# Graph attention on one core: the edge mask multiplied into the centred scores ahead of the exponentials, instead of uniform weights added by products of their own

## What is computed

```python
q = (x @ Wq + bq).reshape(N, H, HEAD)
k = (x @ Wk + bk).reshape(N, H, HEAD)
v = (x @ Wv + bv).reshape(N, H, HEAD)
scores = jnp.einsum('nhd,mhd->nhm', q, k) / np.sqrt(HEAD)
adj = jnp.zeros((N, N), jnp.float32).at[edge_index[0], edge_index[1]].set(1.0)
scores = jnp.where(adj[:, None, :] == 0, -1000000000.0, scores)
attn = jax.nn.softmax(scores, axis=1)
attn_out = jnp.einsum('nhm,mhd->nhd', attn, v).reshape(N, D_OUT)
attn_out = attn_out @ Wo + bo
h1 = _layer_norm(x + attn_out, g1, be1)
ff = jax.nn.relu(h1 @ W1 + b1) @ W2 + b2
```

## Time and profile before

| | before |
|---|---|
| device time, median of 3 runs | 234.52 us (234.5 to 235.0) |
| device time of the profiled execution | 235.3 us |
| its span, first to last instruction | 232.4 us |
| PE busy | 222.9 us, 96% |
| DVE busy | 176.1 us, 76% |
| ACT busy | 127.1 us, 55% |
| POOL busy | 5.5 us, 2% |
| mean granted TensorE clock | 0.995 |

### The profile page before, as it was taken

The page is one execution under the profiler, slowest core; times in us unless marked ns, Lnnn a source line. Parts: engine busy times, 40 slices in busy tenths (PEclk is TensorE's granted clock), DMA queues, the critical chain, the costliest instruction groups (busy, mean ns, idle before and its releaser), DMA issues.

```text
span 232.4 us, 3302 instructions
## 1 busy us (share of the span) xinstructions
PE 222.9 (96%) x1212; PEld 181.1 (78%) x1212; DVE 176.1 (76%) x318; ACT 127.1 (55%) x236; POOL 5.5 (2%) x17
## 2 busy tenths in 40 slices
PE   8999999999999999999999999999999999999970
PEld 4985789766766887888888888888888888997860
DVE  2979776767697689875976868878879767987564
ACT  0646489449679636635546646447476544732320
POOL 1000010000000000000000000000000000001001
PEclk9999999999999999999999999999999999999997
DMA  6999999985003927136100000058840000000001
GB/s 219 323 406 395 394 387 405 404 342 185 0 0 127 400 48 119 31 52 110 21 1 3 0 0 1 0 192 315 283 161 0 0 3 1 0 3 0 0 0 45
DMA packets 28614, 31.25 MB, mean 134 GB/s; under 512 B 17948, under 2 KB 18868, under 8 KB 27576
## 3 DMA queue, kind: packets, MB, share of 16 engines
q1 hardware_dynamic: 27808, 30.54, 38.7%
q10 hardware_dynamic: 792, 0.51, 0.8%
HBM read 30.79 MB, written 0.26 MB: 134 GB/s over the span
## 4 chain that ended last, share of the span: by engine, by line
PE 92%; ACT 3%; DVE 1%; issue 1%; POOLq 0%; POOL 0%; DVEq 0%; ACTq 0%
PE bank L745 37%; PE bank L728 13%; PE bank L544 6%; PE bank L535 6%; PE bank L576 4%; PE bank L593 3%; PE bank L755 3%; PE bank L756 3%; ACT C L342 3%; PE bank L620 2%; PE bank L886 1%; PE bank L553 1%; PE bank L704 1%; PE bank L605 1%; PE bank L705 1%
## 5 line engine op out<-in xcount | busy, mean ns | idle before, releaser
L745 PE MATMUL bank<-W2hi,Hhi 128*128 128x512 f32 x128 | 49.8, 389 | 0.0
L745 PE MATMUL bank<-W2hi,Clo 128*128 128x512 f32 x128 | 49.8, 389 | 0.0
L745 PE MATMUL bank<-W2lo,Hhi 128*128 128x512 f32 x128 | 49.8, 389 | 0.0
L435 ACT ACTIVATE Mhi<-M 128x512 fp32r<-128x512 f32 x32 | 20.3, 633 | 44.2 <-DVE M L1142 44.2
L1147 DVE TENSOR_TENSOR Mlo<-M,Mhi 128x512 fp32r<-128x512 f32 x32 | 22.1, 690 | 11.8 <-ACT M L436 11.8
L1142 DVE TENSOR_TENSOR M<-bank,b2r 128x512 f32<-128x512 f32 x32 | 22.0, 687 | 9.5 <-PE bank L756 5.4
L745 PEld LDWEIGHTS bank<-W2hi,Clo 128*128 128x128 f32 x128 | 24.0, 188 | 5.0
L745 PEld LDWEIGHTS bank<-W2hi,Hhi 128*128 128x128 f32 x128 | 24.0, 188 | 5.0
L745 PEld LDWEIGHTS bank<-W2lo,Hhi 128*128 128x128 f32 x128 | 24.0, 188 | 5.0
L428 ACT ACTIVATE Hhi<-C 128x512 fp32r<-128x512 f32 x32 | 20.0, 624 | 11.4 <-DVE C L1128 11.1
L342 ACT ACTIVATE C<-bank,cols 128x512 f32<-128x512 f32 x32 | 19.5, 704 | 10.5 <-PE bank L576 10.5
(11 more groups left out here) (253 smaller groups left out, 337.8 us busy)
## 6 DMA issues: line engine op xcount, KB each, us to landing
F<-in_L_gnn_W SPq DMA_DIRECT2D x2, 2048.0 KB, 19.3
W<-in_L_gnn_W SPq DMA_DIRECT2D x3, 1024.0 KB, 5.4
W1raw<-in_L_gnn_W SPq DMA_DIRECT2D x1, 2048.0 KB, 22.4
ids<-in_src SPq DMA_DIRECT2D x2, 1024.0 KB, 13.0
ids<-in_dst SPq DMA_DIRECT2D x2, 1024.0 KB, 7.1
dst_ids<-in_dst SPq DMA_DIRECT2D x2, 1024.0 KB, 7.6
src_ids<-in_src SPq DMA_DIRECT2D x1, 2048.0 KB, 8.4
Wq<-in_L_gnn_Wq SPq DMA_DIRECT2D x4, 256.0 KB, 3.9
```

What stands on the lines that cost most here:

```text
L435: act.activation(Mhi[:, t, :], M[:, t, :], ACT.Mish)
L745: done = mm(ST2[t][:, :], x[:, c, e], w[:, c, :], start=c == 0 and i == 0, stop=c == KC - 1 and i == 2)
```

## The change

The product of ones and the mask takes the place of the separate uniform weights. The centred scores are multiplied by min(count, 1) before the exponentials: a pair without an edge has eight scores of 0, eight exponentials of 1, a sum of 8 and eight weights of 1/8. `uniform`, `eighth`, the memset, the ACT instruction and the four products with `uniform` go; so does the mask in L1042. The bias products of L637 move ahead of the wait on `v_ready`.

```diff
             act.activation(CTs[:, :], bank[0][:, 0:N], ACT.Copy).then_inc(S["ct_read"], 1)
-            act.wait_ge(S["eighth"], 1)
-            act.activation(uniform[:, :], bank[0][:, 0:N], ACT.Relu, bias=eighth[:, 0:1], scale=-1.0 / HEADS).then_inc(S["uniform_ready"], 1)
             for o in range(2):
                 act.wait_ge(S["s_centred"], o + 1)
...
             turn_features(0)
-
+            for b in range(2):
+                mm(O_BANKS[b][:, 0:D // 2], ones2[:, :], bvo_parts[:, D + D // 2 * b:D + D // 2 * (b + 1)], start=False, stop=False)
             pe.wait_ge(S["v_ready"], 1)
-            pe.wait_ge(S["uniform_ready"], 1)
-            for j in range(KC):
-                mm(quarter(bank[3], j), v_sb[:, P * j:P * (j + 1)], uniform[:, :], start=j == 0, stop=False)
             for o, j in ((o, j) for o in range(2) for j in range(KC)):
                 h = 2 * j + o
                 pe.wait_ge(S["attn_ready"], o + 1)
                 done = mm(bank[3][HEAD * o:HEAD * (o + 1), P * j:P * (j + 1)], v_sb[:, HEAD * h:HEAD * (h + 1)], attn[:, o, j, :],
-                          start=False, stop=j == KC - 1)
+                          start=j == 0, stop=j == KC - 1)
             done.then_inc(S["ao_done"], 1)
-            for b in range(2):
-                mm(O_BANKS[b][:, 0:D // 2], ones2[:, :], bvo_parts[:, D + D // 2 * b:D + D // 2 * (b + 1)], start=False, stop=False)
...
             for o in range(2):
-                v.tensor_tensor(attn[:, o], bank[1 + o][:, :].rearrange("p (j n) -> p j n", j=KC),
-                                total[:, :].unsqueeze(1).to_broadcast([P, KC, N]), ALU.subtract).then_inc(S["s_centred"], 1)
+                centred = v.tensor_tensor(attn[:, o], bank[1 + o][:, :].rearrange("p (j n) -> p j n", j=KC),
+                                          total[:, :].unsqueeze(1).to_broadcast([P, KC, N]), ALU.subtract)
+            chain(centred)
+
+            dve.wait_ge(S["ct_read"], 1)
+            chain(v.tensor_scalar(mask[:, :], CTs[:, :], 1.0, None, ALU.min))
+            for o in range(2):
+                v.tensor_tensor(attn[:, o], attn[:, o], mask[:, :].unsqueeze(1).to_broadcast([P, KC, N]), ALU.mult).then_inc(S["s_centred"], 1)
...
             chain(v.reciprocal(total[:, :], total[:, :]))
-            dve.wait_ge(S["ct_read"], 1)
-            chain(v.scalar_tensor_tensor(out=total[:, :], in0=CTs[:, :], scalar=1.0, in1=total[:, :], op0=ALU.min, op1=ALU.mult))
             for o in range(2):
                 v.tensor_tensor(attn[:, o], attn[:, o], total[:, :].unsqueeze(1).to_broadcast([P, KC, N]), ALU.mult).then_inc(S["attn_ready"], 1)
```

More of the change, by code:

```diff
@@ L79, in gnn_kernel @@
         warm = sb("warm", [P, P], BF16)
-        uniform = sb("uniform", [P, N])
-        eighth = sb("eighth", [P, 1])
         Dg = sb("Dg", [P, GT, N], F32R)
@@ L206, in gnn_kernel @@
                      "out_stored consts ident_ready x_transposed xT_ready cols_done cols_ready q_done k_done v_done "
-                     "qk_ready v_ready onehot_bf ct_done ct_read uniform_ready eighth ea_done ea_hi ea_lo wc_hi wc_lo bvo_in bvo_hi bvo_parts sign_ready scores_done s_centred exp_done attn_ready ao_done ao_hi ao_lo wo_hi wo_lo wo_done "
+                     "qk_ready v_ready onehot_bf ct_done ct_read ea_done ea_hi ea_lo wc_hi wc_lo bvo_in bvo_hi bvo_parts sign_ready scores_done s_centred exp_done attn_ready ao_done ao_hi ao_lo wo_hi wo_lo wo_done "
                      "stat_ready rstd_ready nx_ready nT_done nT_ready f1_done ff_ready f2_done pre_done pre_read late_done late_read "
@@ L314, in _ @@
             pool.memset(mhalf[:, :], -0.5).then_inc(S["consts"], 1)
-            pool.memset(eighth[:, :], 1.0 / HEADS).then_inc(S["eighth"], 1)
             pool.wait_ge(S["consts"], 3)
```

## The result

| | before | after |
|---|---|---|
| device time, median of 22 executions each | 235.03 us (234.23 to 236.06) | 235.34 us (234.84 to 237.47) |
| mean of the same 22 | 235.01 us | 235.94 us |
| profiled execution: device time, span | 235.3, 232.4 us | 235.5, 233.5 us |
| PE busy, DVE busy | 222.9, 176.1 us | 222.1, 177.3 us |

What follows compares the result with a forecast made beforehand. PE was taken to bound the kernel, reached at the attention through ACT's copy of v and the uniform products. DVE's +1.66 - 0.33, less 0.59 slack, plus 0.06 hand-over, gave +0.80: 235.3 us, range 234.7 to 235.9.

Steps and rivals of the forecast that it cites:

- The mechanism inside the span: Attention: added DVE mask work makes weights 1.33 us later and the heads' products on PE 0.80 us later.
- 0.1 more for a cold start of PE: Heads' products: 0.1 us extra when PE resumes behind its new idle stretch.
- upper bound: Attention: half 1 of the weights late by 0.2 us plus 0.1 for PE's cold start; +1.1, or 235.6 us.
- the delay: Heads' products on PE start 0.80 us later, handed on whole to the end; likeliest case, chance 0.75.
- the first rival: Behind the attention: the delay is taken up on the way, as by fixed transfer waits; about 234.6 us, chance 0.16.
- The faster rival: Attention: without uniform PE could start the heads' products 0.69 us earlier, giving 233.8 us; chance 0.05.
- the last of the sum: Whole kernel: the 0.80 us step added unchanged to the median device time, 234.52 + 0.80 = 235.3 us.
- the rival on the clock: Behind PE's 1.5 us idle stretch: clock falls to 1.2 GHz, +2.7 us on top of 0.80, about 238.0; chance 0.04.

Runs made afterwards that it cites:

- e4: The changed kernel with the four products of v and uniform put back, uniform now all zeros; mean device time 235.81 us.
- e5: The changed kernel without the mask's three DVE instructions, so no pair of nodes is masked; mean 233.95 us, ratio to before 0.9948.
- e2: The changed kernel, unchanged, run again beside before; mean device time 236.41 us, ratio 1.0056.
- e1: The kernel before, unchanged, run again as the measure of scatter; mean device time 235.21 us.
- e3: The changed kernel with six matmuls of ones issued while PE waits for the attention weights; mean device time 235.80 us.
- e6: The changed kernel without the softmax maximum, the mask multiplying the scores straight from the banks; mean 234.87 us, ratio to before 0.999.
- e7: The changed kernel without the softmax maximum, and with edges counted ahead of the products for the scores; mean 234.31 us, ratio to before 0.9961.
- e9: The changed kernel with three matmuls of ones issued while PE waits for the attention weights; mean device time 236.18 us.
- e10: The changed kernel with the product by the mask made twice; mean device time 237.74 us.
- e8: The changed kernel without the maximum, edges counted first, and the mask formed before DVE waits for the scores; mean 233.93 us, ratio to before 0.996.

## Why the prediction was right and where it was wrong

**The mechanism inside the span** was right at each station. The times of after, with its 0.26 of late start taken off, against the forecast: exponentials from 18.65 (18.73), reciprocal to 21.48 + 0.95 - 0.26 = 22.17 (22.25), weights from 22.20 (22.28), heads' products from 23.04 (23.03), aoThi from 24.68 (24.65), the feed-forward products from 32.90 (32.9). Two terms were off and cancelled. The mask took 0.23 us, not 0.29, and the two hand-overs around it 0.03 each, not 0.04; the hand-over from DVE to the waiting PE took 0.14, not 0.06. That 0.08 more is all that the runs show of the "0.1 more for a cold start of PE" in the upper bound, for which the prediction had no row. Scores to end grew from 219.0 to 219.85 and the feed-forward products came 0.83 later, where 0.80 was forecast. Nothing behind the scores took the delay up, so the first rival is out as it was put, by a fixed wait on PE's path; e4 shows that the removed products gave nothing back.

**The faster rival** was priced rightly: with no cost on DVE the heads' products start 0.77 earlier (0.69 forecast, e5). Its time, 233.8, came close to e5's 233.95, but by another sum: of the 1.1 us under before's mean 0.3 came from the span's part behind the scores, 0.3 from the time around the span, and the rest, 0.5, is left for the program's start. It also overlooked Wo's landing, which caps the gain.

**The first step that failed** is the last of the sum, "on the median the same step gives 234.52 + 0.80 = 235.3". It hands the 0.80 of the span on to the device time whole, and so puts at nothing, without a reason, what may change around the span and ahead of the scores. The medians of 22 differ by 0.31, and after's lower group is 0.2 above before in the first comparison and level with it in e2's. The time around the span, which no view of the profile holds, is 2.0 in all 34 executions of after and 2.3 to 2.5 on the mean in before: 0.3 to 0.5 back. And after's lower group has a mean span of 233.21, 0.5 to 0.7 above before's means, not 0.83; so some 0.2 to 0.3 must lie ahead of the scores. That is a remainder, which no run isolates, and why the time around the span differs is open too. What the runs do show is that the delay behind the scores is there, 0.83 at the feed-forward products, and that less than a quarter of it is left in the lower group's device time.

**The second step that failed** is the rival on the clock, given a chance of 0.04 on the evidence that "at the end of the kernel PE has no work from 225 on, and the granted clock is still 1.00 in the stretch 229 to 230". That is one execution. In e1, the same kernel, PE's last work ends before 226, and the clock falls in the stretch from 228:

```profile
225.00:226.00 1.00, 0.65 (x6) 0.44 (x4) 0.48 (x2) 0.00 (x0) 0.00 (x0) 1.00 0.00 0
...
227.00:228.00 1.00, 0.00 (x0) 0.00 (x0) 0.96 (x2) 0.00 (x0) 0.54 (x1) 1.00 0.00 0
228.00:229.00 1.00, 0.00 (x0) 0.00 (x0) 0.96 (x2) 0.00 (x0) 0.00 (x0) 0.71 0.00 0
```

So the delay from the last work to the fall varies by 2 us and more between executions of one program. (It is also why before has mean clocks of 0.988 to 0.990 in some executions. In e1's profile, 0.990, the low level from 228.4 to the end accounts for all that is missing, and it hits no matmul.) The place of that rival was right. Its price, +2.7 us, was too high: 0.95 and 0.9 in the two traces that show the fall, 1.9 to 2.0 between the groups. In e2 the fall comes after PE has resumed, so the heads' products take 2.44 us and not twice 1.60, and part of the low level lies in PE's wait for aoThi. Its chance should have been near 0.4 for each execution. It is no alternative to the delay either: it comes on top, in some executions. It adds 15/34 x 1.9 = 0.8 us to after's mean span, as much as the delay itself.

**Luck.** The forecast 235.3 met the median 235.34 because it started from 234.52, the median of the first three times, whose like over 22 is 235.03. And on the means +0.93 looks like the forecast +0.80 only because the two failed steps nearly cancel: +0.83 behind the scores, +0.7 from the clock (8/22 x 2.0), 0.3 to 0.5 back around the span, and the remainder, 0.1 to 0.3 back, ahead of the scores.

## What to carry to other kernels

An instruction that leaves PE may have been what kept its clock up. Before taking products away from ahead of a wait, work out how long PE then stands still and what dense work comes behind; if the wait can't be shortened, cheap products in the gap (e3, e4) keep the clock up. Here they brought the mean from 236.4 (e2) to 235.8, not the whole of what the clock cost, since the time around the span grew by 0.5 to 0.6. Judge a stall of this kind by many executions and look at their spans and clocks one by one, since a single profile shows one of two outcomes. And work that moves from an engine with slack to the one about to be waited for costs its whole time less the slack: here 1.33 less 0.59, and the hand-over that the slack had hidden. Check besides that a delay of the span arrives in the device time: here the lower group kept 0.0 to 0.2 of 0.83.

## What the runs showed of the hardware that was not expected

- By spans and mean clocks, an idle stretch of 1.57 us on PE was followed by the lower granted clock in 15 of 34 executions, 2.90 us in 4 of 6, stretches of 0.17 to 0.86 us in none of 57 (e3, e4, e6, e7, e9). A trace shows the fall itself once for each of the first two. The fall comes after PE has resumed, in e2 in the stretch 24 to 25, half a microsecond and more behind the resumption at 23.59, in e10 at the end of 25 to 26, with PE back since 24.58. The Trainium skill, TensorE: Matmul & The Clock Gate, section "What's actually happening", calls the activity window free-running, not tied to the kernel's start; the trace agrees in so far as one program at one place does both.
- Device time less span is 1.95 to 2.07 us in every execution of after, e2, e5, e6, e7, e8 and e10 (83 executions), whose PE lists hold the same number of matmuls, 1204; it varies from 2.0 to 3.7, mean 2.3 to 2.6, in before, e3, e4 and e9, with 1207 to 1212. e3 differs from after in PE's list alone. Why the length of that list, or where something comes to lie by it, should matter isn't settled here.
- PE's start behind a wait on DVE costs 0.14 us after an idle stretch (22.46 + 0.70 to 23.30), where 0.04 was seen at 26.51 with PE just out of work.
